# Routing by pairs of tiles, with a table laid out by position, in a decoder layer on one core

## The reference, cut to what matters

```python
logits = x_flat @ gate_weight.T
scores = jax.nn.sigmoid(logits)                     # [4096, 64]
sfc = scores + e_bias[None, :]
group_scores = jax.lax.top_k(sfc.reshape(T, 8, 8), 2)[0].sum(-1)
...                                                 # best 4 of 8 groups, then the best 8 of their experts
topk_w = topk_w / (topk_w.sum(-1, keepdims=True) + 1e-20)      # times 2.5
...
xe = jnp.zeros((E, CAP, H), x.dtype).at[sorted_e, pos].set(tok_sorted, mode='drop')     # CAP = 512
h = jax.nn.silu(jnp.einsum('ech,efh->ecf', xe, w1)) * jnp.einsum('ech,efh->ecf', xe, w3)
ye = jnp.einsum('ecf,ehf->ech', h, w2)
...                                                 # weighted sum over a token's experts
shared = jax.nn.silu(x @ shared_gate.T) * (x @ shared_up.T) @ shared_down.T
```

## Time and profile before

| | us |
|---|---|
| median of 3 runs | 3635.91 (3630.8 to 3637.6) |
| profiled execution | 3647.32, its span 3645.4 |
| PE busy | 3178.9 (87%) |
| DVE busy | 2199.4 (60%) |
| POOL busy | 1557.1 (43%) |
| ACT busy | 1384.6 (38%) |

### The profile page before, as it was taken

How to read it: one execution, slowest core, us unless ns; L and a number is a source line. 1 busy time by engine, 2 the same in 40 slices (tenths; PEclk the granted TensorE clock), 3 DMA queues, 4 the chain that set the end, 5 groups by cost and what they waited for, 6 DMA issues and landing times. The chain is left out here.

```text
span 3645.4 us, 63837 instructions
## 1 busy us (share of the span) xinstructions
PE 3178.9 (87%) x18593; PEld 2049.0 (56%) x18593; DVE 2199.4 (60%) x4889; ACT 1384.6 (38%) x3155; POOL 1557.1 (43%) x1113
## 2 busy tenths in 40 slices
PE   7998989999898998989796999997988883999991
PEld 4444444444445444454344777774767762888880
DVE  4645556564554645556253888885566663777775
ACT  1443434444353443435221666663000000454441
POOL 3342434424243342425431333342466564566661
PEclk8998999999999999999898999998999996999995
DMA  4122121222202122120372212212322112789986
GB/s 119 39 67 71 33 71 36 68 71 67 72 21 79 39 67 71 47 59 3 120 264 90 62 62 68 62 62 75 76 55 52 51 50 84 222 252 248 254 252 211
DMA packets 188692, 343.99 MB, mean 94 GB/s; under 512 B 36153, under 2 KB 53946, under 8 KB 187450
## 3 DMA queue, kind: packets, MB, share of 16 engines
q1 hardware_dynamic: 132282, 242.51, 23.8%
q0 software_dynamic: 28800, 48.43, 5.9%
q10 hardware_dynamic: 27392, 50.34, 3.7%
HBM read 206.96 MB, written 83.89 MB: 80 GB/s over the span
## 5 line engine op out<-in xcount | busy, mean ns | idle before, releaser
L544 ACT ACTIVATE sa_probs<-sa_s 128x512 f32<-128x512 f32 (+3 forms) x1280 | 614.9, 537 | 744.6 <-PE sa_s L435 413.1
L329 POOL TENSOR_TENSOR sa_both<-sa_probs 128x2048 f32<-128x2048 f32 (+2 forms) x160 | 589.9, 3687 | 692.2 <-PE sa_pv L462 680.7
L401 PE MATMUL sa_w<-sa_parts 96*128 96x512 f32 (+3 forms) x1280 | 518.4, 457 | 115.7 <-DVE sa_pmax L603 35.9
L435 PE MATMUL sa_s<-sa_parts 128*128 128x512 f32 (+3 forms) x1280 | 460.0, 410 | 18.9 <-ACT sa_probs L544 13.6
L607 DVE TENSOR_REDUCE sa_pmax<-sa_w 128x1 f32<-128x512 f32 (+3 forms) x768 | 419.1, 584 | 86.3 <-PE sa_w L401 83.0
L401 PEld LDWEIGHTS sa_w<-sa_parts 96*128 96x128 f32 x1280 | 237.9, 196 | 408.1 <-DVE sa_pmax L603 120.7
L603 DVE CUSTOM_DVE_ANT_0 sa_w<-sa_w,sa_maskS 128x512 f32<-128x512 f32 (+3 forms) x512 | 326.2, 649 | 229.9 <-PE sa_w L401 223.7
L1385 POOL DMA_INDIRECT token_and_weight_of_slot<-rt_entry,rt_sl x256 | 254.8, 995 | 151.2 <-DVE rt_entry L1554 75.9
L435 PEld LDWEIGHTS sa_s<-sa_parts 128*128 128x128 f32 x1280 | 244.3, 195 | 130.5 <-ACT sa_probs L544 64.4
L453 PE MATMUL sa_pv<-sa_probs,sa_values 128*32 128x512 f32 (+3 forms) x2560 | 274.7, 548 | 0.0
L1202 ACT ACTIVATE xa_sm<-xa_sm,xa_nmax 128x154 f32<-128x154 f32 x512 | 208.8, 410 | 64.4 <-DVE xa_nmax L1146 64.4
(11 more groups left out here) (243 smaller groups left out, 5821.9 us busy)
## 6 DMA issues: line engine op xcount, KB each, us to landing
ex_w<-in_w SPq DMA_DIRECT2D x138, 512.0 KB
sa_parts<-sa_halves SPq DMA_DIRECT2D x384, 128.0 KB, 2.4
sa_xt<-in_xT SPq DMA_DIRECT2D x32, 1024.0 KB
scratch_attention_T<-sa_oT SPq DMA_DIRECT2D x32, 256.0 KB, 2.2
on_at<-scratch_attention_T SPq DMA_DIRECT2D x32, 256.0 KB, 3.3
on_xr<-in_x SPq DMA_DIRECT2D x32, 256.0 KB, 3.4
scratch_x<-on_xn ACTq DMA_DIRECT2D x32, 256.0 KB, 2.1
scratch_x_T<-on_xnT ACTq DMA_DIRECT2D x32, 256.0 KB, 3.4
```

What stands on the lines that cost most here:

```text
L329: pool.tensor_tensor(both[:, :, 0:w], probs[:, even, :, 0:w], probs[:, odd, :, 0:w], ALU.add).then_inc(both_ready, 1)
L401: nc.tensor.matmul(ps[:, 0:w], qparts[0:3 * HD, h, q0:q0 + P], kparts[0:3 * HD, h, k0:k0 + w], start=True, stop=True).then_inc(work_ready, 1)
L435: mm = nc.tensor.matmul(ps[:, 0:w], kparts[:, h, kb * P:(kb + 1) * P], qparts[:, h, q0:q0 + w], start=True, stop=not diag)
L544: nc.scalar.activation(probs[:, r % NPB, h, 0:w], sbank[n % NSB][:, 0:w], ACT.Exp).then_inc(exp_done, 1)
```

## The change

Routing goes over 16 pairs of tiles. The products `gg`, `uu` and `dd` are done in three float32r terms, with 256 tokens a matmul for the first two, so ACT and DVE split x (`xh`), the hidden layer (`hTh`) and, once, the three weights. On DVE the order in a pass becomes place(p), choose(p+1), hidden(p+1), low_x(p+2), finish(p), low_hidden(p+1). The weights no longer go into the table: `wn` holds all 64 of a token, 8 of them nonzero, and is written beside x2, whose rows grow from 512 to `ROW` = 576 words; the experts take their factor from the gathered row. A slot becomes position x 64 + expert, and a table entry one word. The new table is read without PE transposes. The diff, cut:

```diff
+ROW = DM + E_
...
-                    pool.wait_ge(eq_done, t + 1)
-                    wait(pool, w8_done, t)
-                    pool.tensor_tensor(oh[:], eq[:], wden[:, s].unsqueeze(1).broadcast_to([P, 8, E_]), ALU.mult).then_inc(oh_done, 1)
...
+                    pool.tensor_copy(entry[:, s], tokall[:, bass.ds(p * 2, 2)]).then_inc(tok_done, 1)
+                    pool.wait_ge(tok_done, p + 1)
+                    pool.wait_ge(slot_done, p + 1)
                     apart(pool, passed)
+                    for j in range(2):
+                        for k in range(TOPK):
+                            pool.indirect_dma_start(out=table, out_offset=bass.IndirectOffsetOnAxis(ap=sl[:, s, j, k:k + 1], axis=0),
...
+                def up(p):
+                    pe.wait_ge(xl_done, p * 2 + 2)
+                    for half in range(2):
+                        wait(pe, hT_done, p * 2 + (half - 1))
+                        for n, (w, o, done) in enumerate(((wgh, gg[half], gg_done), (wuh, uu[half], uu_done))):
...
+                            for f in range(2):
+                                c = (2 * half + f) * P
+                                for k in range(KT):
+                                    for i, (a, b) in enumerate(TERMS):
+                                        mm = nc.tensor.matmul(o[:, f * W2:(f + 1) * W2], w[:, a, k, c:c + P], xh[:, b, k],
...
+                def down(p):
+                    pe.wait_ge(hl_done, p * 2 + 2)
...
+                        for n, (a, b) in enumerate(TERMS):
+                            for f in range(KT):
+                                mm = nc.tensor.matmul(dd[j][:], hTh[:, a, f, j * P:(j + 1) * P], wdh[:, b, f],
...
+                def high_x(p):
+                    act.wait_ge(xT_in, p * 16 + 16)
+                    wait(act, uu_done, p * 2)
+                    for j in range(2):
+                        nc.scalar.copy(xh[:, 0, :, j * P:(j + 1) * P], xT[:, j]).then_inc(xh_done, 1)
...
+                def high_hidden(p, half):
+                    act.wait_ge(hT_done, p * 2 + (half + 1))
+                    wait(act, dn_done, p * 2)
...
+                    step(dve.tensor_scalar(ki[:], eight, -1.0, None, ALU.add))
+                    step(dve.tensor_scalar(ki[:], ki[:], 12, None, ALU.logical_shift_right))
+                    step(dve.tensor_scalar(kf[:], eight, float(E_), -float(E_), ALU.mult, ALU.add))
+                    step(dve.tensor_scalar(ef[:], ki[:], 1.0 - float(KEYS * E_), None, ALU.mult))
...
+                def body(p, s):
+                    locate(p, s)
+                    if more(p, 1):
+                        choose(p + 1, 1 - s)
+                        for half in range(2):
+                            hidden(p + 1, half)
+                    if more(p, 2):
+                        low_x(p + 2)
+                    finish(p, s)
+                    if more(p, 1):
+                        for half in range(2):
+                            low_hidden(p + 1, half)
...
-                pool.tensor_copy(factor[:, s], weight[:, bass.ds(unit * J, J)]).then_inc(factor_set, 1)
+                pool.wait_ge(xe_in[s], turn_of(w, s) * (16 * J))
+                apart(pool, passed)
+                pool.tensor_copy(factor[:, s], xe[:, s, :, bass.ds(unit // UPE + DM, 1)].rearrange("p j c -> p (j c)")).then_inc(factor_set, 1)
```

More of the change, by code:

```diff
@@ L1312, in route_and_shared, with more, pair_rows @@
+        def more(p, ahead):
+            return not isinstance(p, int) or p + ahead < NPR
+        def pair_rows(dram, p):
+            return dram[bass.ds(p * W2, W2), :].rearrange("(n p) d -> p n d", p=P)
         with nc.Block() as block:
@@ L1412, in rank @@
-                def rank(t, s):
-                    pe.wait_ge(sel_done, t + 1)
-                    if not isinstance(t, int) or t > 0:
-                        pe.wait_ge(cum_done, t)
-                    wait(pe, kk_done, t * 2)
-                    nc.tensor.matmul(pps[:, 0:E_], tri[:], selb[:, s], start=True, stop=False)
-                    nc.tensor.matmul(pps[:, 0:E_], ones[:], cum[:, s], start=False, stop=True).then_inc(pos_done, 1)
-                def down(t, s):
-                    pe.wait_ge(hT_done, t + 1)
-                    if isinstance(t, int) and t == 0:
-                        pe.wait_ge(w_in, 16)
-                    wait(pe, r_done, t - 1)
-                    for k in range(KT):
-                        mm = nc.tensor.matmul(dd[s][:], hT[:, s, k], wd[:, k], start=k == 0, stop=k == KT - 1)
-                    mm.then_inc(dn_done, 1)
@@ L1429, in _, with score @@
[L1429 to L1435 removed]
+                def score(p):
+                    pe.wait_ge(xT_in, p * 16 + 16)
+                    wait(pe, sc_done, p)
+                    for j in range(2):
+                        for k in range(KT):
+                            mm = nc.tensor.matmul(gps[:, j * E_:(j + 1) * E_], xT[:, j, k], gate[:, k], start=k == 0, stop=k == KT - 1)
+                    mm.then_inc(gate_done, 1)
@@ new lines, in rank @@
+                def rank(p):
+                    pe.wait_ge(sel_done, p + 1)
+                    wait(pe, cum_done, p * 2)
+                    wait(pe, kk_done, p * 2 - 1)
+                    for j in range(2):
+                        o = pps[:, j * E_:(j + 1) * E_]
+                        nc.tensor.matmul(o, tri[:], selb[:, j], start=True, stop=False)
+                        if j == 1:
+                            nc.tensor.matmul(o, ones[:], selb[:, 0], start=False, stop=False)
+                        mm = nc.tensor.matmul(o, ones[:], cum[:], start=False, stop=True)
+                    mm.then_inc(pos_done, 1)
@@ new lines, in _, with body @@
+                high_x(1)
+                for half in range(2):
+                    high_hidden(0, half)
+                def body(p, s):
+                    if more(p, 1):
+                        gates(p + 1, 1 - s)
+                        for half in range(2):
+                            sigmoid(p + 1, half)
+                    if more(p, 2):
+                        high_x(p + 2)
+                    if more(p, 1):
+                        for half in range(2):
+                            high_hidden(p + 1, half)
+                    act.wait_ge(r_done, p * 2 + 2)
+                    act.dma_start(pair_rows(res, p), r[:, s]).then_inc(r_out[s], 16)
```

420 lines of the change are left out of this document (217 added, 203 removed).

## The result

The changed kernel takes 3696.2 us (median of 4 runs, 3693.3 to 3697.5), the kernel before beside it 3633.4 (4 runs): a ratio of 1.0171, 95% interval 1.0151 to 1.019. It is slower by 63 us. The forecast was 3563, its range 3498 to 3618.

The account below looks back on a forecast made before the run. Routing was taken as bounded by GpSimd's scatter ring and a disturbed TensorE, the experts by TensorE. From 3635.9 us, -74 in routing and +1 in the experts gave 3563 us, range 3498 to 3618.

Parts of the forecast that it names:

- the 4.3 us of idle time per sixteen scatters: Routing: TensorE's idle time per pair of tiles in the kernel before, assumed to stay 4.3 us after the change.
- the term for the pair period: Routing: a pair of tiles falls from 30.1 to 25.5 us, so first to last scatter shrinks by 74 us.
- the 9 that I had named as a sign of being wrong: Routing: TensorE idle over 9 us a pair would show the prediction wrong.
- the 20.7 plus 0.5 for lower clock: Routing: TensorE's work per pair falls from 24.7 to 20.7 us, with 0.5 us allowed for lower clock.
- rival 3: Routing: TensorE's signals stay unheard during sixteen scatters, later work queues behind; 33 us a pair, +39, 3676 us; chance 0.17.
- the scatter ring: Routing before: scatters, GpSimd's `oh` multiply and VectorE's sum wait on each other, 13.2 to 14 us a tile.
- 21.4: Routing: GpSimd's time per pair, sixteen scatters in a row, a small copy and the start, 21.4 us.
- the four new subtractions a pair cost POOL nothing: Routing: VectorE's four added subtractions don't lengthen GpSimd's scatters; by the skill's lock rule, 2.8 us a pair instead.
- 16.8: Routing: VectorE's work per pair would be 16.8 us, below TensorE and GpSimd.
- Order: Routing: VectorE places a pair before choosing for the next, so GpSimd starts about 6 us sooner after `rank`.
- Experts: Expert stage: thicker gathers hidden, +3 us taken for them, -2 for dropped transposes and wait, so +1 us.
- rival 1: Routing: scatters alone bound it, 21.4 us a pair, -135, 3502 us; chance 0.22, including 0.04 for stretched scatters.

Follow-up runs that it names:

- two_waits: Changed kernel, but GpSimd waits between a pair's two tiles until the first eight scatters have landed: 3595.8 us, ratio 0.9891.
- four_waits: Changed kernel, but GpSimd waits for the scatters so far to land after each four: 3614.2 us, ratio 0.9939.
- half_scatters: Changed kernel with four scatters a tile instead of eight, half of the table's entries left out: 3558.1 us in one run.
- pairs_f32: Changed kernel with all its copies and waits, but products in one float32 term instead of three float32r terms: 3653.8 us, ratio 1.0051.
- before_again: The kernel before, unchanged, profiled on a chip without the hold: 3612.6 us, ratio 1.0006.
- after_third: Changed kernel, unchanged, run once more on a chip without the hold: 3523.3 us, ratio 0.9764 to the kernel before there.
- after_again: Changed kernel, unchanged, run again on a chip without the hold: 3521.5 us, ratio 0.9757 to the kernel before there.
- choose_first: Changed kernel with VectorE's old order, choosing for the next pair ahead of placing this one: 3529.7 us, ratio 0.9776; repeats 3529.0 and 3532.4.
- late_signals: Changed kernel, but the four signals of the two large products come with the last two matmuls of `up`: 3702.9 us, ratio 1.0199.
- more_matmuls: Changed kernel with 32 extra small matmuls adding zero, spread over the two large products: 3541.0 us; repeat 3540.1 us, ratio 0.9813.
- A to E: Letters of the five follow-up sets, each on one chip beside the kernel before: 3632 and 3637 us in A and B, 3607 to 3611 in C to E.
- short_pauses: Changed kernel with a GpSimd multiply of 320 columns (about 0.9 us) after each four scatters, no wait for landings: 3589.1 us, ratio 0.9943.
- three_waits: Changed kernel, but GpSimd waits for landings twice a pair, leaving runs of five, six and five scatters: 3582.3 us, ratio 0.9919.

## Why the prediction was wrong

The step that failed: "The number of scatters is the same, so I let the 4.3 us of idle time per sixteen scatters stand", in the term for the pair period, 25.5 us. Measured were 33.7, with 9.3 us of idle time for the 4.3 (over the 9 that I had named as a sign of being wrong), and 24.4 us of work for the 20.7 plus 0.5 for lower clock; undisturbed the work is 18.7 (below), so lower clock and the slow stretch itself took 5.7. The idle time is not per scatter. Where PE is held, it has about 50 matmuls from a burst's first scatter and then some one a microsecond until 1.5 us after the last. In the kernel before, whose matmuls are longer on the mean, PE is free again 2 to 3 us after that point; with a burst of sixteen, met by 96 short matmuls, 15 us after it. Cutting the burst (two_waits, four_waits, half_scatters) and making the matmuls fewer (pairs_f32) both take idle time away. I had rows for both halves of this: the gap near the eighth scatter, and rival 3's "one such pause in place of two". I gave it 0.17.

The same 4.3 us was also the wrong price without the hold: 3.1 of it are there in before_again too (PE is busy 355.45 of 400 us, a pair takes 28.3), as waiting for the scatter ring. There the forecast of -2.0% comes near the measured -2.4%, and 3521.5 us lies in the range, but by luck: a pair took 22.1 us and not 25.5, and the kernel before lacked the 36.9 us of hold that I had counted as part of what could be saved.

- *PE*: 20.7 us a pair was too much. Undisturbed it is 18.7 by the rows of after_third: 24 matmuls in 2.8 us, so 0.117 and not the experts' mean of 0.1285, 5.6 for down, 1.9 for scores and ranks.
- *POOL*: 21.4 was 0.7 us short: 350.5 us are 15 x 22.1 + 19.2. "By these rows the four new subtractions a pair cost POOL nothing" was a misreading. The median scatter stays at 0.972 us, but 30 of the 256 of after_again take over 1 us, up to 1.495, 9 us more in all, 0.6 a pair. DVE and POOL there:

```profile
2782.27 0.69 DVE L1584 TENSOR_TENSOR rt_hT<-rt_hg,rt_uu 128x512 f32<-128x512 f32 x1
2782.42 0.97 POOL L1405 DMA_INDIRECT scratch_token_of_slot<-rt_entry,rt_sl  x1 [0.30 <-issue]
2782.87 1.29 DVE L1544 TENSOR_TENSOR rt_xh<-rt_xT,rt_xh 128x512 fp32r<-128x512 f32 x2
2783.70 1.31 POOL L1405 DMA_INDIRECT scratch_token_of_slot<-rt_entry,rt_sl  x1 [0.30 <-issue]
2785.27 1.28 DVE L1588 TENSOR_TENSOR rt_hTh<-rt_hT,rt_hTh 128x512 fp32r<-128x512 f32 x2
2785.31 1.50 POOL L1405 DMA_INDIRECT scratch_token_of_slot<-rt_entry,rt_sl  x1 [0.30 <-issue]
```

  Of 26 scatters that start while a subtraction (L1544, L1588, both operands in SBUF) has 0.15 us or more to go, 25 are longer; of 34 that start so beside L1581, L1584 or L1638, which read one operand from PSUM, none is. 28 of the 30 long ones end 0.84 to 0.85 us after a DVE operation that was under way at their start. The Trainium skill, SBUF — State Buffer, section "SBUF: two separate sides", has a DVE operation with two SBUF inputs lock a GpSimd operation that reads SBUF out for the whole instruction; these rows agree. The 2.8 us a pair that I had worked out by it is too much, since most scatters don't start beside a subtraction. The kernel before had it already, in the earlier trace rows as the longest of 1467 ns and here beside `rt_eq`, a comparison of two operands in SBUF:

```profile
2858.18 0.69 DVE L1529 TENSOR_TENSOR rt_eq<-rt_kk,rt_k 128x512 f32<-128x512 f32 x1
2858.26 1.47 POOL L1385 DMA_INDIRECT token_and_weight_of_slot<-rt_entry,rt_sl  x1 [0.30 <-issue]
```

- *DVE*: 16.8 was high; it was never the bound. Busy time of after_again from 2600 to 2900 us, 184.41 for DVE, 13.6 a pair:

```profile
2600.00:2900.00 300.00, 266.70 (x1893) 248.48 (x1891) 184.41 (x816) 50.54 (x93) 222.50 (x231) 0.93 0.25 74
```

- *Order*: POOL was to start 6 us sooner after the ranks. Without the hold it is worth little: choose_first is 7.5 and 9 us slower over the whole kernel, and first to last scatter takes only 2 us more (352.5 and 352.8 us against 350.5 and 351.1), 0.1 a pair. With the hold it was not measured.
- *Experts*: +1 predicted, +5.2 on the first chip, +3.1 between before_again and after_again (479.1 against 476.0): a small term, and too small.
- *Rivals*: with the hold it came out as rival 3, with 33 us a pair (33.7 measured) and first to last scatter 514 (524.9). Its mechanism was half right: signals do stay out until the burst ends, but late_signals shows that it is PE's pace that costs; down was late because PE reached it late, and it ran at a lower clock. Without the hold it is rival 1, 21.4 us a pair (22.1 measured).

What stays open: which part of the chip holds PE. The profile calls the gaps issue. A count of about 50 matmuls, with as many weight loads, whatever their length, looks like a stock of instructions that isn't refilled while scatters are issued; that is argued from the counts, and no row shows it. The run meant to test the count, more_matmuls, came twice without the hold. Open too is whether the kind goes with the chip or with the time of a run: as far as traces show, all kernels of a set were of one kind, A to E were on five different chips, and no chip was seen at two times.

## What to carry to other kernels

A row of idle time on PE labelled issue, near the end of a row of indirect DMAs, is a warning about the length of such rows: before joining two of them, ask what PE does in the second half. A pause of 2 us between eight and eight scatters won 100 us in one kind of set (between two chips of that kind) and cost 25 in the other; one of 1.1 to 1.2 us didn't end the hold. And profile the kernel before on each chip that a verdict rests on: here its own time (3632 to 3637, or 3607 to 3611) told which kind it was, and with it the sign of the change. And don't read a median where a few long instructions are the question: the longest and the count over 1 us had what the median of the scatters hid.

## What the hardware showed that I had not expected

- Scatters of POOL, 1.28 us apart, let PE start about 50 matmuls and then one a microsecond, in three of six sets of runs. Fewer entries per scatter (64 partitions) made it worse: 36.3 us a pair instead of 33.7, in one run and on another chip.
- A pause of 1.1 to 1.2 us in the scatters let the hold go on in four places of four (two_waits); after about 2 us or more PE had its 50 or so matmuls again.
- A scatter that starts beside a DVE operation on two SBUF operands ends 0.84 us after that operation, up to 1.50 us instead of 0.97; beside one with an operand in PSUM it keeps its time.
- The hold is paid twice: the granted clock fell to 0.50 in it, and the 24 matmuls of down behind it took 8.92 us instead of 5.76.
- A pause with POOL busy on 320 columns after each four scatters (short_pauses, 3589.1, three pauses a pair) costs about as much as two waits for landings (three_waits, 3582.3), without the hold.
